# The cluster layer computed inside the grouped-query attention's block, tile by tile, with its last residual sum on GpSimd

## What is computed

```python
dots = softmax(x @ centroids.T / 0.1)            # 64 clusters
hits = dots > 0.01
query_sel = any(hits, axis=1)                    # per row
cluster_sel = any(hits, axis=0)                  # per cluster, over ALL rows
row_sel = cluster_sel[assignments]               # per output column
dense = x @ weight.T + bias
out = where(query_sel[:, None] & row_sel[None, :], dense, 0)
x = layernorm(x + out)
```

## Time and profile before

| what | value |
|---|---|
| median of 3 runs | 2520.19 us (2520.02 to 2528.79) |
| profiled execution | 2533.18 us, span 2530.8 us |
| busy, whole span | PE 2471.5 us (98%), DVE 1555.9 us (61%), ACT 1392.1 us (55%), POOL 1134.9 us (45%) |
| PEclk (granted TensorE clock in tenths of full speed) | 9 in nearly all of 40 slices, 8 in the first and last |
| the last merge's addition to X | 2463.92 us |
| `column` copied (L1827) | 2499.90 us |
| last normalised tile written | 2526.53 us |

### The profile page before, as it was taken

The page is one execution under the profiler, slowest core; times in us unless marked ns, Lnnn a source line. Parts: engine busy times, 40 slices in busy tenths (PEclk is TensorE's granted clock), DMA queues, the critical chain, the costliest instruction groups (busy, mean ns, idle before and its releaser), DMA issues. The chain is left out here.

```text
span 2530.8 us, 40532 instructions
## 1 busy us (share of the span) xinstructions
PE 2471.5 (98%) x12630; PEld 1861.0 (74%) x12630; DVE 1555.9 (61%) x2790; ACT 1392.1 (55%) x2155; POOL 1134.9 (45%) x1140
## 2 busy tenths in 40 slices
PE   8999999999999999999998999899999999999997
PEld 4677777777777777777775688778888888888874
DVE  6666666666666666666664522375756657557556
ACT  3677777777777777777776432232423424324231
POOL 1556555555555565556554243243434334334210
PEclk8999999999999999999999999999999999999998
DMA  6122222222222222222221422111001010010001
GB/s 213 42 45 55 45 53 47 51 53 44 53 46 57 46 53 44 53 46 54 45 53 38 139 88 88 65 44 42 17 25 41 0 41 17 25 41 17 1 3 52
DMA packets 47611, 125.38 MB, mean 50 GB/s; under 512 B 6034, under 2 KB 23442, under 8 KB 41427
## 3 DMA queue, kind: packets, MB, share of 16 engines
q1 hardware_dynamic: 47570, 124.85, 18.5%
HBM read 80.27 MB, written 10.49 MB: 36 GB/s over the span
## 5 line engine op out<-in xcount | busy, mean ns | idle before, releaser
L427 DVE TENSOR_REDUCE row_max<-ps_max 128x1 f32<-128x512 f32 x1024 | 670.4, 687 | 196.7 <-PE ps_max L517 174.9
L292 POOL TENSOR_TENSOR p_parts<-probs,p_parts 128x1024 f16<-128x1024 f32 x256 | 547.6, 2148 | 369.0 <-ACT p_parts L346 368.1
L341 ACT ACTIVATE probs<-ps_score 128x1024 f32<-128x1024 f32 x512 | 523.1, 1022 | 240.4 <-PE ps_score L533 218.6
L531 PE MATMUL ps_score<-Q,K 128*128 128x512 f32 x1024 | 408.1, 398 | 2.1 <-ACT probs L341 2.1
L533 PE MATMUL ps_score<-Q,K 97*128 97x512 f32 x1024 | 406.7, 397 | 0.0
L517 PE MATMUL ps_max<-KX,Q 68*128 68x512 f32 x1024 | 378.8, 411 | 2.2 <-DVE row_max L427 2.1
L421 DVE TENSOR_TENSOR Q<-ps_x,Q 64x512 fp32r<-64x512 f32 x254 | 175.1, 689 | 242.5 <-ACT Q L336 238.8
L346 ACT ACTIVATE p_parts<-probs 128x1024 f16<-128x1024 f32 x256 | 269.4, 1053 | 4.0
L517 PEld LDWEIGHTS ps_max<-KX,Q 68*128 68x128 f32 x1024 | 189.6, 190 | 75.0 <-issue 28.1
L531 PEld LDWEIGHTS ps_score<-Q,K 128*128 128x128 f32 x1024 | 194.2, 190 | 61.7 <-ACT probs L341 13.5
L533 PEld LDWEIGHTS ps_score<-Q,K 97*128 97x128 f32 x1024 | 195.0, 190 | 39.4
(11 more groups left out here) (269 smaller groups left out, 4387.6 us busy)
## 6 DMA issues: line engine op xcount, KB each, us to landing
Q<-Q SPq DMA_DIRECT2D x64, 512.0 KB, 4.3
ffn_raw<-in_w_ffn SPq DMA_DIRECT2D x22, 768.0 KB, 4.4
w_raw<-in_w_qrope SPq DMA_DIRECT2D x32, 512.0 KB, 3.6
wq_raw<-in_wq SPq DMA_DIRECT2D x8, 1024.0 KB, 5.5
wo_raw<-in_wo SPq DMA_DIRECT2D x8, 1024.0 KB, 4.8
content_k<-probs SPq DMA_DIRECT2D x8, 512.0 KB, 6.4
Q<-content_q SPq DMA_DIRECT2D x64, 64.0 KB
K<-content_k SPq DMA_DIRECT2D x64, 64.0 KB
```

Source lines behind the costliest of these rows:

```text
L292: pool.tensor_tensor(p_lo[:, j, :, :], probs[:, j, 0:PAIRED, :], p_hi[:, j, :, :], ALU.subtract)\
L341: act.activation(probs[:, j, 2 * half:2 * half + 2, :], ps_score[half][:, :, :], ACT.Exp, scale=SCALE).then_inc(exped, 1)
L427: dve.tensor_reduce(row_max[:, t, j:j + 1], ps_max[t % 2][:, :], axis=AXX, op=ALU.max)\
L531: pe.matmul(ps_score[half][:, k, :], K1[:, b, t * P:(t + 1) * P], Q1[:, b, j, :], start=True, stop=False)
```

## The change

Steps 2 to 4 above are no blocks of their own any more. Their instructions are appended to the engines' programs inside `gqa_stage`'s block, and merges 0 to 7 of the last pass move there as well. The PSUM banks are those of the attention (7 banks in place of the 4 for the turned X and 7 for the cluster stage), and most SBUF tiles are laid over buffers of the attention that are free by then. In detail:

- TensorE: merges 0, 1, `outputs`, 2; then X tile t is turned between the merges, two to three tiles behind; the logits of the first half come between the turning of tile 4 and merge 7; dense tiles 0 to 4 fill the time of the softmax; there are five banks for dense tiles in place of four, two banks in place of four for the turned X.
- VectorE: each tile has its own `bn_aggr`, reciprocal and `tensor_scalar`, straight behind its sum; the softmax is done in two halves, each VectorE instruction on 256 elements per partition in place of 512. Behind `column`, the normalisation of tile t-2 stands between the work of tiles t-1 and t.
- ScalarE: a square root per tile; `high_x(t-2)` stands behind the root of tile t. A load of the Exp table stands between `high_x(5)` and `high_x(6)`, one of the Sqrt table behind the second half's Exp.
- GpSimd: splits centroids, bias and the low part of the weight (one `tensor_tensor` of 128 x 2048) in place of VectorE, and does `X += dense` of all eight tiles.
- SyncE: the loads are issued in the last pass, as soon as their buffers are free; a tile is stored when it is normalised.

The core of the diff (the old stages' removal, buffers and semaphores left out):

```diff
         @block.gpsimd
...
             run(pool, body)
+            pool.wait_ge(turned, 3 * NU * NKV)
...
+            pool.memset(ones[:, :], 1.0).then_inc(set_up, 1)
...
+            pool.iota(which[:, :], pattern=[[0, 1]], base=0, channel_multiplier=1,
+                      allow_small_or_imprecise_dtypes=True).then_inc(set_up, 1)
...
+            pool.tensor_copy(ch, cent).then_inc(cl_step, 1)
...
+            pool.tensor_tensor(cl, cent, ch, ALU.subtract).then_inc(cl_ready, 1)
...
+            pool.tensor_copy(ones_r[:, :], ones[0:1, :]).then_inc(cl_step, 1)
...
+            pool.tensor_copy(bias_h, bias).then_inc(cl_step, 1)
...
+            pool.tensor_tensor(bias_l, bias, bias_h, ALU.subtract).then_inc(cl_ready, 1)
...
+            pool.tensor_copy(assign, assign_i).then_inc(cl_step, 1)
...
+            pool.wait_ge(w_high, 1)
+            pool.tensor_tensor(wl, w_raw, wh, ALU.subtract).then_inc(cl_ready, 1)
+            for t in range(TT):
+                pool.wait_ge(dense_taken, t + 1)
+                pool.tensor_tensor(X[:, t, :], X[:, t, :], dense[:, t % 2, :], ALU.add).then_inc(dense_added, 1)
         @block.scalar
...
+            def root(t, base):
+                act.wait_ge(mean_var, base + t + 1)
+                act.activation(dev[:, t:t + 1], moments[:, t, 1:2], ACT.Sqrt, bias=eps[:, 0:1]).then_inc(rooted, 1)
...
+            act.activation(wh, w_raw, ACT.Copy).then_inc(w_high, 1)
+            act.wait_ge(eps_set, 3)
+            act.activation(unused[:, :], eps[:, :], ACT.Sqrt)
+            root(0, x_base)
+            take_outputs(KV, NU - 1)
+            root(1, x_base)
+            for t in range(2, TT):
+                root(t, x_base)
+                high_x(t - 2)
+                if t == TT - 2:
+                    take_logits(0)
+            act.activation(unused[:, :], eps[:, :], ACT.Exp)
+            high_x(TT - 2)
+            high_x(TT - 1)
+            exp_soft(0)
+            take_logits(1)
+            exp_soft(1)
+            act.activation(unused[:, :], eps[:, :], ACT.Sqrt)
+            for t in range(TT):
+                root(t, x_base + TT)
         @block.vector
...
+            def aggregate(t, base):
+                dve.bn_stats(sb["stats"][:, t, :], X[:, t, :]).then_inc(counted, 1)
+                dve.wait_ge(counted, base - x_base + t + 1)
+                dve.bn_aggr(moments[:, t, :], sb["stats"][:, t, :]).then_inc(mean_var, 1)
+
+            def sum_out(t):
+                dve.wait_ge(made, START + PER * KV + ring_out(True, t) + 1)
+                dve.tensor_tensor(X[:, t, :], out_bank(t)[:, :], X[:, t, :], ALU.add).then_inc(taken, 1)
+                dve.wait_ge(taken, merged(t))
+                aggregate(t, x_base)
+
+            def norm(t, base):
+                at = base - x_base + root_base + t + 1
+                dve.wait_ge(rooted, at)
+                dve.reciprocal(dev[:, t:t + 1], dev[:, t:t + 1]).then_inc(inverse_set, 1)
+                dve.wait_ge(inverse_set, at)
+                dve.tensor_scalar(X[:, t, :], X[:, t, :], moments[:, t, 0:1], dev[:, t:t + 1],
+                                  ALU.subtract, ALU.mult).then_inc(x_normed, 1)
+
+            def low_x(t):
+                dve.wait_ge(x_high, x_base + t + 1)
...
+            def finish(t):
+                dve.wait_ge(dense_added, t + 1)
+                aggregate(t, x_base + TT)
...
+            sum_out(0)
+            norm(0, x_base)
+            sum_out(1)
+            low_o(LAST, NU - 1)
+            norm(1, x_base)
+            for t in range(2, TT):
+                sum_out(t)
+                low_x(t - 2)
+                norm(t, x_base)
+            low_x(TT - 2)
+            low_x(TT - 1)
+            shift_logits(0)
+            take_hits(0)
+            shift_logits(1)
+            take_hits(1)
...
+            after(dve.tensor_copy(column, ps_h[:, :]))
+            for t in range(TT):
+                dve.wait_ge(dense_made, t + 1)
+                if t >= 2:
+                    dve.wait_ge(dense_added, t - 1)
+                dve.scalar_tensor_tensor(out=dense[:, t % 2, :], in0=d_banks[t % ND][:, :], scalar=hit[:, t:t + 1],
+                                         in1=column, op0=ALU.mult, op1=ALU.mult).then_inc(dense_taken, 1)
+                if t:
+                    finish(t - 1)
+                if t >= 2:
+                    norm(t - 2, x_base + TT)
+            finish(TT - 1)
+            norm(TT - 2, x_base + TT)
+            norm(TT - 1, x_base + TT)
         @block.tensor
...
+            merge(True, tk, 0)
+            merge(True, tk, 1)
+            outputs(LAST, NU - 1)
+            merge(True, tk, 2)
+            for t in range(TT - 3):
+                turn_x(t)
+                if t == 0:
+                    merge(True, tk, 3)
+                    pe.wait_ge(o_low, ONE + LAST + 1)
+                    continue
+                if t == ST:
+                    pe.wait_ge(cl_ready, 1)
+                    logits(0)
+                merge(True, tk, t + 3)
+            turn_x(TT - 3)
+            turn_logits(0)
+            turn_x(TT - 2)
+            pe.wait_ge(cl_ready, 3)
+            dense_tile(0)
+            turn_x(TT - 1)
+            dense_tile(1)
+            logits(1)
+            dense_tile(2, 0, 6)
+            turn_logits(1)
+            dense_tile(2, 6)
+            dense_tile(3)
...
+            dense_tile(4, 0, 6)
+            pe.wait_ge(onehot_made, 1)
+            pe.matmul(ps_h[:, :], ones[0:NCL, :], onehot, start=True, stop=True).then_inc(column_made, 1)
+            dense_tile(4, 6)
+            for t in range(5, TT):
                 dense_tile(t)
```

More of the change, by code:

```diff
@@ L718, in _ @@
                                   ALU.subtract, ALU.mult).then_inc(normed, 1)
[L719 to L724, removed]
+            for t in range(TT):
+                dve.wait_ge(high, base + t + 1)
+                dve.tensor_tensor(sb["xl"][:, :, t * P:(t + 1) * P], turned[t % 4][:, :, :],
+                                  sb["xh"][:, :, t * P:(t + 1) * P], ALU.subtract).then_inc(low, 1)
+            dve.wait_ge(low, base + TT)
         @block.scalar
@@ L731, in _ @@
             act.activation(dev[:, :], moments[:, :, 1], ACT.Sqrt, bias=eps[:, 0:1]).then_inc(rooted, 1)
[L732 to L736, removed]
+            for t in range(TT):
+                act.wait_ge(x_turned, base + t + 1)
+                act.activation(sb["xh"][:, :, t * P:(t + 1) * P], turned[t % 4][:, :, :], ACT.Copy).then_inc(high, 1)
         @block.tensor
         def _(pe):
[L740 to L747, removed]
+            for t in range(TT):
+                pe.wait_ge(normed, base + t + 1)
+                if t >= 4:
+                    pe.wait_ge(low, base + t - 3)
+                for c in range(DC):
+                    last = pe.transpose(turned[t % 4][:, c, :], X[:, t, c * P:(c + 1) * P], ident[:, :])
+                last.then_inc(x_turned, 1)
         @block.sync
         def _(sp):
[L751 to L758, removed]
+            ahead(sp)
 RAW = 3
@@ L1690, in _ @@
             run(pe, body)
[L1693 to L1708, removed]
@@ L1845, in _, with turn_x, logits @@
+            def turn_x(t):
+                pe.wait_ge(x_normed, x_base + t + 1)
+                if t >= 2:
+                    pe.wait_ge(x_low, x_base + t - 1)
+                for c in range(DC):
+                    last = pe.transpose(x_banks[t % 2][:, c * P:(c + 1) * P], X[:, t, c * P:(c + 1) * P], ident[:, :])
+                last.then_inc(x_turned, 1)
+            def logits(b):
+                pe.wait_ge(x_low, x_base + (b + 1) * ST)
                 k = 0
@@ new lines, in dense_tile @@
+            def dense_tile(t, begin=0, end=2 + 3 * DC):
+                out = d_banks[t % ND][:, :]
+                if begin == 0:
+                    pe.wait_ge(x_low, x_base + min(t + (2 if t in (3, 4) else 0), TT - 1) + 1)
+                    if 1 <= t <= 2:
+                        pe.wait_ge(taken, merged(TT - 3 + t))
+                    if t >= ND:
+                        pe.wait_ge(dense_taken, t - ND + 1)
+                steps = [(ones_r[:, :], part) for part in (bias_h, bias_l)]
+                steps += [(x[i][:, c, t * P:(t + 1) * P], (wh, wl)[j][:, c, :]) for i, j in TERMS for c in range(DC)]
+                for k in range(begin, end):
+                    last = pe.matmul(out, *steps[k], start=k == 0, stop=k == len(steps) - 1)
+                if end == len(steps):
+                    last.then_inc(dense_made, 1)
```

324 lines of the change are left out of this document (157 added, 167 removed).

## The result

| | before | after |
|---|---|---|
| timed, median of 16 runs each | 2523.60 us (2518.65 to 2528.79) | 2516.24 us (2511.40 to 2520.96) |
| profiled execution, its span | 2533.18 us, 2530.8 us | 2519.56 us, 2517.5 us |
| first sum of the last pass to the end of the span | 88.1 us | 76.5 us |

The ratio of the timed runs is 0.9971, 95% interval 0.9962 to 0.9980: 7.3 us faster (5.0 to 9.6), where 13.5 us were forecast and 2506.7 us named. 2516.24 us lies outside the range of 2503 to 2512. The 2506.7 us were counted from the median of 3 runs, 2520.19 us; the kernel before has 2523.60 us over 16 runs, and 3.4 us of the distance of 9.5 come from that. The two profiled executions, though, are 13.6 us apart and their spans 13.3 us. What follows asks why the timed gain is so much smaller.

The account below looks back on a forecast made before the run. TensorE was 98% busy, but the edited end was taken as bound by VectorE's handovers, then TensorE, then VectorE held by GpSimd. The span's end moved from 2530.8 to 2517.3 us, 13.5 us less: 2506.7 us, range 2503 to 2512.

Parts of the forecast that it names:

- Up to X tile 2: Last pass's first merges and norms: nothing won; norm(0) just precedes GpSimd's long subtraction, norm(1) waits, tile 2 costs 0.2 us.
- rival 1: GpSimd's long weight subtraction comes before norm(0)'s `tensor_scalar`; tile 2 starts 2.5 us later, gain 11.0 us, 2509.2 us; chance 0.20.
- Tiles 2 to 7: Last pass's X tiles: the VectorE and ScalarE handover sets the pace, 3.83 us per tile, or 3.74 if the root frees earlier.
- TensorE's floor: Tiles 2 to 7: a merge and four transposes keep TensorE busy 3.2 us per tile, the least a turn can take.
- The pause and the clock: Ahead of the first half's logits: TensorE waits 1.6 us, from 2463.7 to 2465.3 us, then runs at full clock.
- Rival 4: First logits to `column`: TensorE's clock falls in new pauses and stays low for 98 matmuls, 20.6 us, 2527.3 us; chance 0.05.
- Logits to `column`: From the first logits to the copy of `column`: TensorE alone sets the time, 28.8 us, copy at 2494.1 us.
- `column` to the end: Last normalisation and stores: VectorE, held by GpSimd's sums, sets turns of 2.35 us; the span ends at 2517.3 us.
- The sum: Whole kernel: span 2530.8 less 2517.3 us gives 13.5 us, taken off the median to name 2506.7 us.
- rival 2: Half clock at the first logits belongs to the profile; absent in timed runs, gain 10.2 us, 2510.0 us; chance 0.12.
- TensorE's hole of 4.5 us: Kernel before, between the last merge at 2463.9 and 2468.4 us: no TensorE work, said to be in every execution.

Follow-up runs that it names:

- merge7_first: The kernel after, with merge 7 and the turning of tile 5 ahead of the first half's logits; 2516.17 us against 2526.46 for the kernel before.
- high_first: The kernel after, with ScalarE's `high_x(t-2)` ahead of the root of tile t; 2513.27 us against 2525.13 for the kernel before.
- sum_dve: The kernel after, with the last residual sum back on VectorE instead of GpSimd; 2520.13 us against 2526.46 for the kernel before.
- wl_split: The kernel after, with GpSimd's subtraction for the weight's low part in four 128x512 pieces; 2514.25 us against 2526.46 for the kernel before.
- after_1: The kernel after, unchanged, timed once and profiled in a further execution; 2517.97 us.
- after_2: The kernel after, unchanged, timed once and profiled in another further execution; 2513.02 us.
- all3: The kernel after, with wl_split, merge7_first and high_first together and `take_logits(0)` behind the last root; 2514.81 us against 2525.13 for the kernel before.
- before_2: The kernel before, unchanged, timed once and profiled in a further execution; 2518.55 us.
- before_warm: The kernel before, with idle TensorE transposes, 28 ahead of the turning of X and 16 behind it; 2526.39 us against 2526.51 for the kernel before.

## Why the prediction was wrong

**Up to X tile 2: wrong, rival 1 held.** GpSimd was forecast to be through with its small instructions at 2445.2 and norm(0) to ask at 2444.9. Both came about 1.7 us earlier, with the first sum at 2441.02 in place of 2442.68; corrected for that GpSimd was there at 2444.75, 0.45 us sooner than worked out (its small instructions took 4.8 us, from 2438.27, where 5.5 were estimated), and norm(0) on time (2444.88). The race was seen, priced (2.5 us) and given a chance of 0.20; it was lost by 0.12 to 0.14 us, in all six traces that have the long subtraction (the kernel after three times, merge7_first, high_first, sum_dve). The price was too low: 1.9 us of it, from wl_split's first logits (22.2 us behind the first sum) to 24.1, are the delay, and the clock that falls in the longer pause adds 1.6 (after) to 2.8 us (after_1, after_2), together 3.5 to 4.7.

**Tiles 2 to 7: right.** Turns of 3.83 us forecast, 3.74 measured, the lower of the two ends given; what sets them was the handover to ScalarE, as high_first shows by taking it away. TensorE's floor of 3.2 us was seen in all3.

**The pause and the clock: wrong in size.** 1.6 us of pause were forecast, at full clock behind it. It was 2.5 us, and the clock fell. Rival 4 had the place, not the extent: at 0.21 us each, the lower clock covered 8 matmuls (after) and 14 (after_1, after_2), not 65. It did not fall behind the 1.33 us of wl_split. The argument against this rival, that the clock had fallen before a pause of 4.5 us where the new one would be 1.6, misread the rows: ahead of the slow logits of the kernel before stood a pause of 3.03 us, with the clock at 1.00 before it.

**Logits to `column`: right.** From the first logits to the sum of tile 7 two products of 2.72 us and its handover, 5.7, were in the sum: 5.72 us in wl_split, 7.30 and 8.49 us where the clock fell. From there to `column` 23.1 us were in the sum, and 23.0 were measured. The step's 28.8 us is sound at full clock.

**`column` to the end: right, 1.1 us too long.** 23.2 us forecast, 22.1 measured: six turns 0.04 shorter each, and 2.4 us from the last `tensor_scalar` to the end (2515.08 to 2517.5) where 3.2 were taken; the stores now come 2.3 us apart, as the tiles are normalised. The page "SBUF — State Buffer" of the Trainium skill, section "SBUF: two separate sides", would have made the turn 2.53 us by a lock held for the whole instruction. A `tensor_scalar` of 0.55 us that starts at 2503.05 and ends at 2503.81 can have run from 2503.26, and GpSimd's sum is recorded up to 2503.52: by the measurement the block ends 0.26 us before the recorded end, where the prediction had 0.19. That there is a block agrees, and at its largest here, 4.72 us.

**The sum: the step that failed.** 13.5 us was the forecast end against one profiled execution, "taken off the median". It rested on a tail of 88.1 us before and 74.6 us after. Its two sides, by the other traces of the same stretch:

- Before: 85.0, 86.9, 86.9 us in the other three, 1.2 to 3.1 below 88.1. This is mostly rival 2 (priced at 3.3 us for 16 matmuls; 14 ran at the lower clock, and from the first logits to `column` the first trace took 2.8 us more than before_2), which had 0.12. The prediction argued against it that TensorE's hole of 4.5 us is in every execution. It is, and the clock falls behind it in all four, but that is the fall ahead of the turning of X. The one at the logits follows a second pause, and is missing in one trace and half as long in two.
- After: 76.5, 77.7, 77.7 us, 1.9 to 3.1 above 74.6. This is the lost race with its clock, less the 1.1 us above.

The tails of the kernel before are 86.8 us in the mean of four traces and those of the kernel after 77.3 in the mean of three: 9.4 us apart, inside the timed interval (5.0 to 9.6) but near its upper end. So the traces account for 4.1 of the 6.2 us by which the forecast gain was too large; the other 2.1 lie within the interval and are not explained. Rivals 1 and 2 were held for alternatives of 0.20 and 0.12, although nothing keeps them apart. The first came in full, the second in part; by their own prices the two together leave 13.5 - 2.5 - 3.3 = 7.7 us, 2512.5 us, just outside the range.

The second part of the step is the time from which the gain was taken off: the median of 3 runs, 2520.19 us, where 16 runs have 2523.60. That is 3.4 of the 9.5 us between 2506.7 and 2516.24; the rest is the smaller gain. That the profiled pair gave 13.3 us of span, near the forecast 13.5, proves nothing: 11.6 of it is the tail, the dearest of the kernel before against the cheapest of the kernel after, and 1.7 came in ahead of the edit (2.6 in the start, less 1.0 between there and the first sum). That it came near is luck.

The end of 2517.3 us for the profiled span, measured 2517.5, is right by errors that cancel: 1.7 us earlier at the first sum and 1.1 less at the end, against 3.0 more between first sum and `column`.

**What stays open.** Which share of the timed runs of the kernel before has the half clock at its logits isn't known; the times give a median over starts that differ by 10 us, and before_warm was too coarse to tell. So the 2 us between the traces' 9.4 and the timed gain stay open too. Why the clock in the first 100 us comes back earlier in some executions wasn't tried.

## What to carry to other kernels

Price a change from stretches cut at the same events, and read the stretch in three or four executions of the kernel before: one profile bounds neither its start nor its clock. When a pause is blamed for a fallen clock, read the clock ahead of it too. Where two mechanisms of a forecast are independent, work out the time at which both happen, rather than give each a small chance alone. Before one long GpSimd instruction is placed beside VectorE's work, ask which `tensor_scalar` can meet it; cut in pieces it costs 5.20 us in place of 4.57 on GpSimd and gives VectorE a gap after each. Putting what the other engine waits for first in an in-order queue (high_first) was worth as much in the traces.

## What the runs showed of the hardware

- A 128x512 `tensor_scalar` took 4.72 us beside a 4.57 us subtraction of GpSimd, 1.44 and 1.26 us beside four of 1.28 to 1.46 us, and 0.72 to 0.76 us where it met the last part of a sum of 1.26 to 1.29. In each case it can have begun 0.26 to 0.27 us before the recorded end of GpSimd's instruction, if it ran for its own 0.55. Beside the same four, an addition from PSUM (0.68 us), `bn_stats` (0.69), `bn_aggr` (0.18) and the subtraction of `low_o` (0.69) took what they take without GpSimd.
- After a pause of 2.51 or 2.52 us TensorE's clock was at its lower level in four traces of four (the kernel after three times, sum_dve), and after one of 1.99 us, ahead of the idle transposes of before_warm, it was at 0.54 in the mean from 2461.4 to 2464 us. After 1.33 us (wl_split) and 1.22 us (before_warm) it was at full clock. In the kernel before, pauses of 3.03, 2.87 and 2.87 us ahead of the logits were followed by the lower level, one of 2.98 us (before_2) by full clock: the length of the last pause alone does not decide.
- The sum on VectorE, recorded with 0.66 us, made its turn 0.39 us longer than the sum on GpSimd (2.70 against 2.31 us): the hold of 0.2 us per `tensor_scalar` took back about a third of what the move gave.
